# A graph network on one core: propagation sums turned as two float16 parts, and edge logits computed in other gaps of the preparation

## What is computed

```
L0: h = 0.9 * (sum over edges of h[src]*norm[src]) * norm + 0.1*h0     # ten times
L1: q, k, v of the nodes; per edge and head exp(clip(q.k)) weights, normed sum of v
L2: h @ W_self.T + mean over edges of (weight * h[src]) @ W_neigh.T + biases
L3: ci * sum over edges of sigmoid(edge_attr @ ps_w.T) * (h*cj)[src]
```

## Time and profile before

| | |
|---|---|
| median of three runs | 1531.5 us (1531.42 to 1532.58) |
| profiled execution | 1535.3 us, its span 1533.5 us |
| PE / DVE / ACT / POOL busy | 71% / 69% / 35% / 46% |
| preparation, up to the first matmul of L0 | 0 to 404 us, its first part up to L957 at 270.5 us |
| propagation | 404 to 792 us |
| edge layers | 792 us to the end |

### The profile page before, as it was taken

The page is one execution under the profiler, slowest core; times in us unless marked ns, Lnnn a source line. Parts: engine busy times, 40 slices in busy tenths (PEclk is TensorE's granted clock), DMA queues, the critical chain, the costliest instruction groups (busy, mean ns, idle before and its releaser), DMA issues.

```text
span 1533.5 us, 31745 instructions
## 1 busy us (share of the span) xinstructions
PE 1091.4 (71%) x11999; PEld 880.3 (57%) x11999; DVE 1057.3 (69%) x1275; ACT 535.2 (35%) x1214; POOL 710.0 (46%) x444
## 2 busy tenths in 40 slices
PE   1994638777699999999954677676734666736663
PEld 1993627677455555555533676676634566635663
DVE  6096594799423222322356899999988999579997
ACT  0221101666300000000012766666623555225553
POOL 1000000788888787787888899999700000000000
PEclk9999999655699999999986878788766889659888
DMA  5432101100000000000011634434303333123331
GB/s 100 105 84 75 42 0 42 15 1 1 2 2 2 2 1 1 1 1 2 2 47 12 215 135 156 157 134 166 136 28 117 151 133 113 44 90 134 138 151 22
DMA packets 47059, 105.93 MB, mean 69 GB/s; under 512 B 30900, under 2 KB 31700, under 8 KB 47006
## 3 DMA queue, kind: packets, MB, share of 16 engines
q1 hardware_dynamic: 30380, 89.41, 16.6%
q10 hardware_dynamic: 3025, 14.88, 3.9%
q0 software_dynamic: 13600, 0.92, 3.2%
HBM read 101.68 MB, written 3.03 MB: 68 GB/s over the span
## 4 chain that ended last, share of the span: by engine, by line
DVE 38%; PE 37%; issue 17%; DVEq 2%; SPq 2%; DMA 1%; ACT 1%; another core or an unknown queue 0%; ACTq 0%
PE ps L1355 22%; DVE arena L797 4%; PE ps L1242 4%; DVE hl_room L957 3%; PE ps L1341 3%; DVE arena L747 3%; DVE arena L765 3%; DVE base_room L760 3%; DVE arena L753 3%; DVE arena L788 3%; PE ps L1232 2%; PE ps L1187 2%; DVE arena L844 2%; DVE arena L779 2%; DVE h_room L779 1%
## 5 line engine op out<-in xcount | busy, mean ns | idle before, releaser
L452 POOL DMA_INDIRECT w_table<-wpa,slot_i x425 | 705.4, 1660 | 394.5 <-ACT wpa L559 265.3
L1187 PE MATMUL ps<-arena 125*128 125x64 f16 (+1 forms) x3900 | 266.4, 223 | 199.4 <-DVE arena L797 100.9
L1355 PE MATMUL ps<-arena,hl_room 125*128 125x500 f16 (+1 forms) x1750 | 343.9, 353 | 8.9 <-DVEq L1012 8.9
L1187 PEld LDWEIGHTS ps<-arena 125*128 125x128 bf16 x3900 | 199.7, 108 | 215.2 <-DVE arena L797 90.6
L1355 PEld LDWEIGHTS ps<-arena,hl_room 125*128 125x128 f16 x1750 | 161.3, 99 | 168.5 <-issue 11.4
L1024 DVE TENSOR_TENSOR h_room<-ps,coef 125x256 f32<-125x256 f32 (+1 forms) x70 | 27.7, 396 | 269.6 <-PE ps L1341 233.0
L1202 PE MATMUL ps<-arena 128*128 128x128 f16 (+1 forms) x1950 | 149.6, 245 | 18.6 <-DVE arena L774 9.8
L587 ACT ACTIVATE part_room<-ps 128x500 f32<-128x500 f32 (+1 forms) x70 | 38.0, 543 | 348.2 <-PE ps L1355 321.9
L1202 PEld LDWEIGHTS ps<-arena 128*128 128x128 bf16 x1950 | 138.8, 112 | 20.3 <-issue 20.2
L1192 PE MATMUL ps<-arena 125*128 (+1 forms) x1300 | 149.0, 214 | 0.0
L491 ACT ACTIVATE arena<-ps 128x384 f32<-128x384 f32 x325 | 131.6, 504 | 10.9 <-PE ps L1192 8.9
(11 more groups left out here) (237 smaller groups left out, 1440.7 us busy)
## 6 DMA issues: line engine op xcount, KB each, us to landing
hl_room<-slot_rows SPq DMA_DIRECT2D x100, 832.0 KB, 4.1
hl_room<-in_edge_attr_dram ACTq DMA_DIRECT2D x17, 750.0 KB
w_table<-wpa,slot_i POOLq DMA_INDIRECT x425
xs<-in_x_dram SPq DMA_DIRECT2D x1, 750.0 KB
out_dram<-xs SPq DMA_DIRECT2D x1, 750.0 KB
w_table<-arena SPq DMA_DIRECT2D x1, 650.0 KB, 4.2
part_room<-w_table SPq DMA_DIRECT2D x1, 650.0 KB, 4.1
edge_place<-arena ACTq DMA_DIRECT2D x1, 622.6 KB
```

Of the source, the lines that this page charges most:

```text
L452: pool.indirect_dma_start(w_table, bass.IndirectOffsetOnAxis(slot_i[:, u:u + 1], 0), wpa[:, u], None).then_inc(S[f"w_out{g % 2}"], 16)
L1187: last = pe.matmul(ps[:, m % RING, o:o + b - a], ohT[:, par, 0, k * L:(k + 1) * L], rhs, start=(i == 0), stop=(i == 1))
L1355: last = pe.matmul(ps[:, c, 0:w], hl[0:P, u, s, :], adj[:, s, c * CH * P:c * CH * P + w], start=(s == 0), stop=(s == T - 1))
```

## The change

**Propagation.** The sums are copied as two float16 parts: ScalarE writes the high one, scaled by 1/4096 (`PSCALE`), DVE the remainder (`low_sums`). `pair` is float16, a tile is turned by two accumulating matmuls, and the stationary slices are 128 columns wide, so that three columns behind a group are read; DVE clears the 12 pad columns once. `coef` takes the factor 4096 back. `mains_taken` is now DVE's. DVE does `low_sums` of group n + 1 ahead of the node update of group n, except at the end of an iteration, where the order is the other way round.

**Preparation.** The columns of `psw2` are loaded right behind the indices; the node vectors `cjs`, `cis` go behind the clearing of the table. ScalarE issues the first feature loads only after the indices have landed. In a dot the projection is stationary: `psw2` is 50 columns wide, zero but for two, and a window of 26 columns places the two results of a block in rows of one 26 x 125 sum over the chunk; ScalarE copies it to `zT`, and at the end 17 transposes bring all logits into place. `EA_RUN` becomes 12; the square root comes behind group 43 in ScalarE's program; 12 groups stand between the flag and L1267, and the other 16 in four gaps: behind sort tile 0, ahead of and behind tile 13, and behind the sort. The place table is stored and read back from SP's queue, in two splits each.

```diff
-        EA_RUN, EA_FLAG, EA_SORT = 22, 40, 54
+        EA_RUN, EA_FLAG, EA_STD, EA_SORT = 12, 40, 44, 52
+        EA_BETWEEN = (52, 56, 60, 64)
...
+            sp.wait_ge(S["psw2_clear"], 1)
+                    sp.dma_start(psw2[e * D:(e + 1) * D, CJ - 1 + e:CJ + e], ps_w.rearrange("o f -> f o")).then_inc(S["psw2_in"], 16)
...
             with sp.If(way < 1):
+                for a, b in SPLIT:
+                    sp.dma_start(edge_place.rearrange("(p j) c -> p (j c)", p=P)[a:b], place[a:b].rearrange("p j c -> p (j c)")
+                                 ).then_inc(S["place_out"], 16)
+                sp.wait_ge(S["place_out"], 32)
+                for a, b in ((0, 80), (80, BT * JT)):
+                    sp.dma_start(placed[a:b], edge_place.rearrange("(b r p) c -> r b (p c)", r=BT * JT, p=P)[a:b]).then_inc(S["place_back"], 16)
...
+            def turned_logits(c):
+                act.wait_ge(S["ea_dot"], 4 * (c + 1))
+                act.activation(zT[:, c], ps[0:CJ + 1, 7, 0:P], ACT.Copy).then_inc(S["z_turned"], 1)
...
+            act.wait_ge(S["idx_in"], 64)
             load_features(0)
             load_features(1)
...
-                turned_features(EA_FLAG, EA_SORT)
+                turned_features(EA_FLAG, EA_STD)
             std_of_var(1)
             with act.If(way < 1):
-                turned_features(EA_SORT, len(EA_GROUPS))
-                act.wait_ge(S["ea_dot"], len(EA_GROUPS))
-                act.activation(wpa[:, :, 1], ps[0:P, 7, 0:J], ACT.Sigmoid).then_inc(S["pa_ready"], 1)
+                turned_features(EA_STD, len(EA_GROUPS))
+                turned_logits(J // CJ - 1)
+                act.wait_ge(S["z_back"], 1)
+                act.activation(wpa[:, :, 1], ps[0:P, 5, 0:J], ACT.Sigmoid).then_inc(S["pa_ready"], 1)
...
-                            act.activation(part[:, n % 2, 0:w], ps[:, c, 0:w], ACT.Copy).then_inc(S["mains_taken"], 1)
+                            act.activation(part[:, n % 2, 0, 0:w], ps[:, c, 0:w], ACT.Copy, scale=1 / PSCALE).then_inc(S["part_high"], 1)
...
+                def low_sums(i, n):
+                    vec.wait_ge(S["part_high"], i * (2 * NCH) + (n + 1))
+                    vec.scalar_tensor_tensor(part[:, n % 2, 1, 0:w], ps[:, c, 0:w], 1 / PSCALE, part[:, n % 2, 0, 0:w],
+                                             ALU.mult, ALU.subtract).then_inc(S["mains_taken"], 1)
...
+                def two_iterations(i, more):
+                    for n in range(2 * NCH):
+                        turn = n % NCH == NCH - 1
+                        if turn:
+                            new_nodes(i, n)
+                        if more or n + 1 < 2 * NCH:
+                            low_sums(i, n + 1)
+                        if not turn:
+                            new_nodes(i, n)
...
                 for k in range(n):
-                    j = c * CJ + (first + k) * 2
-                    m = min(2, (c + 1) * CJ - j)
-                    last = pe.matmul(ps[0:P, 7, j:j + m], eaT[0:m * D, g % 2, k * P:(k + 1) * P], psw2[0:m * D, 0:m], start=True, stop=True)
+                    block = first + k
+                    w = min(L, CJ * D - block * L)
+                    at = CJ - 1 - 2 * block
+                    last = pe.matmul(ps[0:CJ + 1, 7, 0:P], psw2[0:w, at:at + CJ + 1], eaT[0:w, g % 2, k * P:(k + 1) * P],
+                                     start=(block == 0), stop=(block == EA_BLOCKS - 1))
...
                     for k in range(min(CH, T - CH * c)):
-                        last = pe.matmul(ps[0:P, 7, k * D:(k + 1) * D], part[:, odd, k * P:(k + 1) * P], pair[:, :], start=True, stop=True)
+                        for e in range(2):
+                            last = pe.matmul(ps[:, 7, k * D:(k + 1) * D], part[:, odd, e, k * P:k * P + L], pair[:, :],
+                                             start=(e == 0), stop=(e == 1))
```

93 lines of the change are left out of this document (55 added, 38 removed).

## The result

The changed kernel takes 1438.98 us (median of 4; 1436.31, 1443.72, 1441.65, 1434.22) against 1531.46 us (1530.65 to 1532.58) on the same chip: a ratio of 0.9396, 95% interval 0.936 to 0.9432. That is 92.5 us less; 104 were forecast. The times of the changed kernel also lie 9.5 us apart, those of before 1.9.

The account below looks back on a forecast made before the run. The prediction took DVE waiting for TensorE to bound the preparation and TensorE alone the propagation. 72.0 + 32.3 - 0.1 = 104.2 us off gave 1427.3 from the median, said as 1428; own range 1414 to 1442, wider 1413 to 1468.

Parts of the forecast that it names:

- The clock: Preparation: the new dots keep TensorE streaming, so it runs at 2.4 GHz, not 1.2; a chunk takes 5.2 us, before 8.09.
- Its rival with the low clock: Preparation: TensorE stays at 1.2 GHz, chunks take 8.3 us, 34.6 us gained there, total 1465; chance 0.16.
- Part 2, the start: Start up to L836: earlier indices and three faster chunks bring L836 45.2 us earlier (40 to 47).
- Part 3: Stretch after the flag, 37.2 us before, shrinks to 19.0: 18.2 us earlier (8 to 20).
- Part 4: Sort: chunks between its tiles cost 3.2 and 6.0 us, 9.2 us later (4 to 15).
- Part 5: Behind the sort: 28.9 us for 14 groups become 11.1, 17.8 us earlier (15 to 20).
- Part 6, the propagation: Propagation: float16 turns at 0.033 us a matmul instead of 0.103, less new waits, 32.3 us earlier (5 to 35).
- the wait of group 5: Propagation: group 5's turn, covered only by group 6, loses 0.3 us in each of 10 iterations (0 to 1.5).

Follow-up runs that it names:

- old_dots: Changed kernel with the dots turned back (features stationary, two projection columns streamed, no back turns), same schedule: 1460.3 us, ratio 0.9534.
- vectors_late: Changed kernel with the two node vectors loaded behind the place table's store and return: 1439.52 us, ratio 0.9393.
- half_scatter: Changed kernel with 215 of the 425 scatter transfers of the slot weights, the other weights left out: 1437.26 us, ratio 0.9367.
- prep_only: The new preparation with the old propagation: 1466.86 us, ratio 0.9548.
- prop_only: The old preparation with the new propagation: 1504.29 us, ratio 0.98.
- pa_early: Changed kernel with the first ten chunks' logits through the sigmoid ahead of the sort, so their scatter starts early: 1432.31 us, ratio 0.9346.
- flag44: Changed kernel with one more chunk (groups 40 to 43) ahead of the flag: 1433.61 us, ratio 0.9346.
- warm_layer: Changed kernel with 90 idle matmuls on TensorE ahead of the first edge layer's projections: 1438.76 us, ratio 0.9393.
- loads_first: Changed kernel with late node vectors, and x, weights and table clearing held until the second chunk has landed: 1442.84 us, ratio 0.9428.
- gaps_behind: Changed kernel with the three chunks in the sort's gaps put back behind the sort: 1445.79 us, ratio 0.9422.
- all_four_70: Changed kernel with one more chunk ahead of the flag, later node vectors, early scatter and 70 idle matmuls: 1423.74 us, ratio 0.9286.

## Why the forecast was near, and where it failed

**The clock** (the main choice) was right. L1268 runs at 0.65 us per four from 18 us on, except behind waits (1.09 at 30.20 and at 97.79), and turning the dots back takes it away and costs 21 us. That the granted clock of 1.00 ahead of 274 us was no measurement is borne out by `old_dots`: 36 records against 54 in equal windows that both say 1.00. Once the clock has changed the row does follow: the changed kernel's says 0.60 from 30 to 36 us. But the clock was worth less than the prediction held. Its rival with the low clock left 34.6 of the preparation's 72.0 us, 37.4 less; `old_dots` keeps 45.4 of 66.0, 20.6 less (the rival also paid some 3 us for back turns, which that run doesn't have). By stage the clock gave 11.7 us up to the flag where the prediction had 19.4, 5.5 for 10.3 from there to L921, 4.8 for 5.8 in the sort, and behind it -1.3 for 1.9. The order of loads and groups by itself was worth more than held, 45.4 for 34.6. That the two errors, 16.8 us too much and 10.8 too little, partly cancel is luck, and a reason why 72.0 came so near to 66.0. The rule weighed beside it, that the full clock doesn't engage for transposes (the Trainium skill, TensorE: Matmul & The Clock Gate, Part 4), does not hold for this stream: 13 of the 39 records of a chunk are transposes, and L1268 itself runs at the higher clock. With the other dots beside them the same transposes ran at the low clock (1.07 at 40.42 in `old_dots`), so the dots make the difference.

**Part 2, the start: 40.35 instead of 45.2.** The failed term is the loads. The first chunk came at 14.70, not 12.5, and the node vectors were priced at 1.5 us; the second of them held the queue for 17.33 us (6.81 in the kernel before, where it was issued at 15.13), the third chunk came 4.08 us late, and the clock fell. `vectors_late` shows this step at 31.46 without them, even under the forecast's 33.1. One reason was wrong as well: the rival with the low clock put L836 at 38.2, and the low-clock kernel has 38.36, while the fast one has 37.92. The forecast clock bought nothing here; it paid at the flag, where seven slow chunks don't fit under VectorE.

**Part 3: 15.6 instead of 18.2.** The chunks behind the flag took 7.3, 6.4 and 5.3 us where 6.6, 5.6 and 5.0 stood, and the 15 turns of L1308 took 2.8 us for 1.8. The clock was high there (granted 1.00 from 113 to 116): they start 0.17 us apart, 0.21 in the kernel before at the low clock. The price of 0.104, taken from another form, was too low; what sets the 0.17 wasn't tested.

**Part 4: 9.0 later, forecast 9.2**, three stalls of 2.99, 2.75 and 3.02 where two of 3 and 6 were foretold. **Part 5: 19.0 instead of 17.8.** Preparation 66.0, forecast 72.0. The 2.4 us of the adjacency can't be put down to the change: the same code takes 121.2 to 121.7 us in `half_scatter`, `prep_only` and `prop_only`, 117.9 to 118.7 in `pa_early` and the changed kernel.

**Part 6, the propagation: 32.4, forecast 32.3.** The turn costs 0.23 us for 8 matmuls, 0.03 each, as read off L1187; the wait of group 5 is 0.19 for the 0.3 forecast.

**The silent step: all that stands behind the propagation was taken to move with it.** It didn't. The scatter's start moved 66 us earlier, with the sigmoid, but the need for its table moved 101.5, from 1157.5 to 1056.0. The 35.5 us between are time at 1.49 us a transfer that is gone, room for 24 (35.5 / 1.49). Counted in the traces: before, 347 transfers start ahead of the first edge layer, 78 in it and none behind; after, 325, 91 and 9. The 13 more inside it cost 3.8 to 5.7 us each. Before, the table's load was issued at 1106.82 and was in by 1110.8, 46.7 us ahead of its need; after, it was in 3.6 us behind it. In the other profiled executions with the new propagation and the scatter where it was, the wait was 0.15 (`flag44`, `old_dots`), 3.19 (`warm_layer`), 4.27 (`loads_first`), 6.82 (`prop_only`), 8.03 (`vectors_late`) and 12.36 (`gaps_behind`). In part this is the step from three transfers per tile to two: it comes after 10 tiles in `gaps_behind`, 11 in `vectors_late`, 14 in the changed kernel and 15 in `old_dots`. Why it comes at all isn't known. Of the median it is 4.4 us by `half_scatter` and 7.7 by `pa_early`, with the noise said above. The page of before showed it: POOL busy at 9 tenths in slices 24 to 28, and a scatter of 705 us on one engine. A sum that counts only the engines of the chain passes it by.

**The median against the profile.** The forecast for the profiled execution's like was 1431.1, measured 1436.31: 5.2 us, the preparation's 6.0 and the scatter's 3.5 less what fell in elsewhere. The other 6.5 us by which the median misses (1438.98 against 1427.3) are only where the profiled executions lie among their kernels' times: that of before is 3.8 above its median, and the forecast took the same for the changed kernel's, which is 2.7 below. What makes the changed kernel's times spread is settled in part. Two terms on its path vary: the wait for the weights (0.15 to 12.4) and the clock at the projections (7.9 us, in one of eleven profiles without idle matmuls ahead of them). Others vary too: with the same start the first-column step comes at 37.92 to 39.83 in seven profiles, and the adjacency varies by 3.8 us. In the kernel before, whose times lie within 1.9 us here and within about 5 us in the seven to nine runs of it on each of the other chips, there is no wait for the weights; why the low clock at the projections doesn't spread its times as well isn't known. `prep_only` has no weights wait and still spreads over 9.2 us, and `all_four_70` too. Whether the clock at the projections makes that up, or something at another stage, is open: each kernel has one profile.

## What to carry over

After a stage is shortened, look for the engines that ran beside it and are awaited behind it: their work doesn't shrink with it, and a table that lay ready 47 us early is late after a gain of 32 in the stage beside it (`prop_only`). Transfers of one element per packet belong where nothing else is loaded; moving them is worth it only if the new place is empty too. TensorE's pace is to be read off equal records (us for four turns); the clock row says 1.00 at either pace until its first change. And when two causes come in one change, turn one back: of 66 us that looked like the clock's, 45 were not.

## What the runs showed of the hardware

- Indirect transfers of GpSimd cost 1.49 us each beside the propagation, but in VectorE's loop of the first edge layer only two or three pass per 11.35 us, single ones taking 7.5 to 9.0 us, each of which ends inside a reduction of VectorE. VectorE isn't slowed: the layer takes 310.9 us with the whole scatter and 311.8 with the half that is over before it.
- The second of two loads of a 3125-element column held its queue for 17.33 us beside other loads, 16.37 beside three chunks, 4.00 with no other load.
- After 16.85 us of idle time TensorE's 25 transposes ran at the low clock (5.42 us for 2.86), and whether the 50 matmuls behind them ran at the high one (8.4 us) or not (16.4 us) differed between executions of nearly the same program.
